# Second attention of a fused convolution-attention kernel: its accumulators move to other PSUM banks, its first blocks run earlier, and two transposed rows are split earlier

## What is computed

```python
def _L1_attn_ref(x):                       # x: tokens after layer norm, (16, 1024, 256)
    xn = x / (jnp.linalg.norm(x, axis=-1, keepdims=True) + EPS)
    scores = jnp.einsum('bid,bjd->bij', xn, xn)
    scores = scores * scores
    weights = jax.nn.softmax(scores, axis=-1)
    context = jnp.einsum('bij,bjd->bid', weights, x)
    return context

x = _L0_conv_ref(x, ...)                   # group norm, q/k/v, softmax attention, projection, residual
t = _to_tokens(x)
t = t + _L1_attn_ref(_ln_t(t))             # the second attention
t = t + _L1_ffn_ref(_ln_t(t), L1_ffn_weight, L1_ffn_bias)
x = _from_tokens(t, x)
```

## Time and profile before

| | |
|---|---|
| median of three runs | 1754.06 us |
| the profiled execution: time, span of its trace | 1754.25 us, 1752.5 us |
| PE busy | 1678.9 us (96%) |
| DVE, ACT, POOL busy | 1359.3, 995.6, 778.3 us |
| mean granted TensorE clock | 0.997 of full speed |
| DMA | 228.40 MB, mean 130 GB/s |

### The profile page before, as it was taken

How to read it: one execution, slowest core, us unless ns; L and a number is a source line. 1 busy time by engine, 2 the same in 40 slices (tenths; PEclk the granted TensorE clock), 3 DMA queues, 4 the chain that set the end, 5 groups by cost and what they waited for, 6 DMA issues and landing times.

```text
span 1752.5 us, 33771 instructions
## 1 busy us (share of the span) xinstructions
PE 1678.9 (96%) x11234; PEld 1527.6 (87%) x11234; DVE 1359.3 (78%) x2597; ACT 995.6 (57%) x1556; POOL 778.3 (44%) x1206
## 2 busy tenths in 40 slices
PE   7999999999999999999999999999999999999996
PEld 6888889888888988889888998888988888898886
DVE  7768777787777877778787777877778777887775
ACT  3565646556465565745647466574655646456572
POOL 1362535526254372634626345253542725337161
PEclk9999999999999999999999999999999999999998
DMA  4634525355252643526344263452535525353342
GB/s 130 168 109 137 154 88 167 103 158 161 82 157 88 191 132 105 150 82 197 112 130 137 92 180 108 144 152 87 162 101 167 156 84 151 99 182 107 109 131 62
DMA packets 197150, 228.40 MB, mean 130 GB/s; under 512 B 27776, under 2 KB 170496, under 8 KB 197120
## 3 DMA queue, kind: packets, MB, share of 16 engines
q1 hardware_dynamic: 197120, 228.01, 43.8%
HBM read 123.08 MB, written 104.86 MB: 130 GB/s over the span
## 4 chain that ended last, share of the span: by engine, by line
issue 27%; POOL 25%; PE 19%; DVE 9%; ACT 8%; DMA 7%; SPq 2%; POOLq 1%; DVEq 0%; ACTq 0%
PE wide L456 10%; POOL e_back L1432 4%; POOL ln_r L1393 4%; POOL prob L1427 3%; DMA e_scratch<-x_norm 3%; DMA e_back<-e_scratch 3%; PE turn L662 3%; POOL val L1419 3%; PE narrow L456 2%; ACT expo L808 2%; POOL xn_lo L1383 2%; PE turn L653 2%; SPq L386 2%; DVE x_norm L1097 2%; DVE prob L1102 1%
## 5 line engine op out<-in xcount | busy, mean ns | idle before, releaser
L456 PE MATMUL wide<-xn_hi,prob 128*128 128x512 f32 x1024 | 305.2, 399 | 3.0 <-DVE prob L1080 3.0
L456 PEld LDWEIGHTS wide<-xn_hi,prob 128*128 128x128 f32 x1024 | 185.2, 188 | 44.7 <-DVE prob L1080 6.3
L815 ACT ACTIVATE prob<-e_back 128x1024 fp32r<-128x1024 f32 x112 | 118.3, 1057 | 144.3 <-DMA e_back<-e_scratch 144.3
L1443 POOL TENSOR_TENSOR carrier_p<-ones 128x1 f32<-128x1 f32 x60 | 11.7, 195 | 417.2 <-DVE y_sb L1185 414.7
L808 ACT ACTIVATE expo<-wide,neg_max 128x1024 f32<-128x1024 f32 x128 | 142.5, 1113 | 73.6 <-DVE neg_max L1090 73.3
L1097 DVE STREAM_TRANSPOSE x_norm<-expo 128x1024 f32<-128x1024 f32 x112 | 139.2, 1243 | 41.7 <-ACT expo L808 41.3
L619 PE MATMUL narrow<-val,prob 128*128 128x258 f32 x512 | 146.7, 287 | 25.9 <-DVE prob L1160 25.9
L1102 DVE TENSOR_TENSOR prob<-e_back,prob 128x1024 fp32r<-128x1024 f32 x112 | 136.1, 1215 | 36.9 <-ACT prob L815 36.9
L1090 DVE TENSOR_REDUCE neg_max<-wide 128x1 f32<-128x1024 f32 x128 | 155.3, 1213 | 11.9 <-PE wide L456 10.0
L1427 POOL TENSOR_TENSOR prob<-expo,prob 128x128 fp32r<-128x128 f32 (+6 forms) x112 | 146.7, 1321 | 39.5 <-DVE prob L1137 39.5
L456 PE MATMUL wide<-xn_lo,prob 128*128 128x512 f32 x512 | 160.7, 394 | 0.0
(11 more groups left out here) (178 smaller groups left out, 5450.9 us busy)
## 6 DMA issues: line engine op xcount, KB each, us to landing
e_scratch<-x_norm SPq DMA_DIRECT2D x112, 512.0 KB, 3.0
e_back<-e_scratch SPq DMA_DIRECT2D x448, 128.0 KB, 3.2
x_raw<-in_x SPq DMA_DIRECT2D x32, 512.0 KB, 3.9
e_back<-in_x SPq DMA_DIRECT2D x64, 256.0 KB, 5.0
out<-y_sb SPq DMA_DIRECT2D x64, 256.0 KB, 3.0
e_scratch<-x_norm SPq DMA_DIRECT2D x32, 448.0 KB, 2.6
x_tok<-e_scratch SPq DMA_DIRECT2D x128, 112.0 KB, 2.6
e_scratch<-x_norm SPq DMA_DIRECT2D x16, 384.0 KB, 2.9
```

Source lines behind the costliest of these rows:

```text
L456: mm = pe.matmul(o, lhsT, r, start=first and i == 0, stop=last and i == len(parts) - 1)
```

## The change

The four accumulators `out2` were the two narrow banks and half of each wide tensor. Now they are the first narrow bank, the two banks of `turn`, and the second narrow bank. The products therefore need no longer wait for the squares that read `wide`, and the next image's queries wait for the squares and not for the residuals.

Three of the pair's 16 blocks ((n, j) = (0, 0), (0, 1) and (1, 1), nine matmuls) run in `front`, between the score pieces 3 and 4. The rest of the pair runs j = 2 to 7, with block (1, 0), the one that reads transposed row 1, just ahead of j = 6.

On ACT, `exp2` is cut into `square2` and `exp2`; the transposed tokens of group 2 (`cosT_hi`) go between the square and the exponential of piece 2, and `e2T_hi` of rows 1 and 2 goes ahead of pieces 7 and 8. On DVE, `e2T_lo` of rows 1 and 2 goes ahead of the splits of row 7. The last image's tail uses other banks for its first half. POOL's and SP's queues keep their order.

```diff
-        out2 = [narrow[0], narrow[1], wide[0][:, 0:BANK], wide[1][:, 0:BANK]]
+        out2 = [narrow[0], turn[:, 0:BANK], turn[:, BANK:N], narrow[1]]
...
-        LAST = dict(ln2T=[turn, wide[1]], y=[y_wide, [narrow[0][:, :], narrow[1][:, :]]], tT=[turn, wide[1]])
+        LAST = dict(ln2T=[wide[1], turn], y=[y_wide, [narrow[0][:, :], narrow[1][:, :]]], tT=[wide[1], turn])
...
-            def product2_pair(b):
-                order = [1, 2, 3, 4, 5, 0, 6, 7]
-                pe.wait_ge(t1_made, NT * b + NT)
-                pe.wait_ge(cosT_made, N1 * b + N1)
+            def products2_begin(b):
+
+                pe.wait_ge(t1_made, NT * b + 6)
+                pe.wait_ge(val_made, N1 * b + 1)
+                pe.wait_ge(p_made, (NT - 1) * b + 2)
+                product2_block(b, 0, 0, 0, 7)
+                product2_block(b, 0, 1, 0, 7)
+                product2_block(b, 1, 1, 1, 7)
+
+            def products2_end(b):
+
                 pe.wait_ge(val_made, N1 * b + N1)
-                for j in order:
-                    if 0 < j < NT - 1:
+                for j in range(2, NT):
+                    if j == NT - 2:
+                        product2_block(b, 1, 0, 1, 7)
+                    if j < NT - 1:
                         pe.wait_ge(p_made, (NT - 1) * b + j + 1)
-                    elif j == NT - 1:
+                    else:
                         pe.wait_ge(p_last_made, 2 * b + 1)
                     for n in (0, 1):
-                        mm = product2_parts(b, n, j, order)
-                        if j == order[-1]:
-                            mm.then_inc(pv2_up, 1)
+                        product2_block(b, n, j, n, 7)
 
             def product2(b, n):
                 if n >= 4:
                     pe.wait_ge(t2_made, NT * b + n - 3)
-                else:
-                    pe.wait_ge(sq2_made, NP * b + NP)
+                elif n == 3:
+                    pe.wait_ge(cosT_made, N1 * b + N1)
...
                 if f is not None:
-                    pe.wait_ge(t2_made, NT * f + NT - 1)
+                    pe.wait_ge(sq2_made, NP * f + NP)
                 queries(b, 0)
-                if f is not None:
-                    pe.wait_ge(t2_made, NT * f + NT)
-                else:
+                if f is None:
                     pe.wait_ge(prep_dve, 8)
                 queries(b, 1)
                 if f is None:
                     pe.wait_ge(prep_dve, 12)
+                else:
+                    pe.wait_ge(t2_made, NT * f + NT)
...
                 scores2(b, 3)
+                products2_begin(b)
                 scores2(b, 4)
...
+                square2(b, 2)
+                cosT_hi(b, 2)
                 exp2(b, 2)
-                cosT_hi(b, 2)
...
+                square2(b, 6)
                 exp2(b, 6)
-                exp2(b, 7)
-                exp2(b, 8)
                 e2T_hi(b, 1)
                 e2T_hi(b, 2)
+                square2(b, 7)
+                exp2(b, 7)
+                square2(b, 8)
+                exp2(b, 8)
...
                 e2_turn(b, 6)
+                e2T_lo(b, 1)
+                e2T_lo(b, 2)
                 e2_hi(b, 7)
                 e2_last_lo(b, 7)
                 e2_hi(b, 8)
                 e2_turn(b, 7)
-                e2T_lo(b, 1)
-                e2T_lo(b, 2)
                 e2_last_lo(b, 8)
```

More of the change, by code:

```diff
@@ L610, in scores2, with product2_block @@
                 three(parts, [wide[J % 2][:, o + s.start:o + s.stop] for s in cuts]).then_inc(s2_up, 1)
-            def product2_parts(b, n, j, order):
+            def product2_block(b, n, j, first, last):
                 if j < n:
@@ L618, in product2_parts @@
                 o = out2[n % 4]
-                pe.matmul(o[:, 0:w], hi, val[:, j, 0:w], start=j == order[0], stop=False)
+                pe.matmul(o[:, 0:w], hi, val[:, j, 0:w], start=j == first, stop=False)
                 pe.matmul(o[:, 0:C], hi, val[:, j, w:w + C], start=False, stop=False, skip_group_check=True)
-                return pe.matmul(o[:, 0:w], lo, val[:, j, 0:w], start=False, stop=j == order[-1])
-            def product2_pair(b):
-                order = [1, 2, 3, 4, 5, 0, 6, 7]
-                pe.wait_ge(t1_made, NT * b + NT)
-                pe.wait_ge(cosT_made, N1 * b + N1)
+                mm = pe.matmul(o[:, 0:w], lo, val[:, j, 0:w], start=False, stop=j == last)
+                if j == last:
+                    mm.then_inc(pv2_up, 1)
+            def products2_begin(b):
[6 more added lines that the diff above has]
+            def products2_end(b):
                 pe.wait_ge(val_made, N1 * b + N1)
-                for j in order:
-                    if 0 < j < NT - 1:
+                for j in range(2, NT):
+                    if j == NT - 2:
+                        product2_block(b, 1, 0, 1, 7)
+                    if j < NT - 1:
                         pe.wait_ge(p_made, (NT - 1) * b + j + 1)
-                    elif j == NT - 1:
+                    else:
                         pe.wait_ge(p_last_made, 2 * b + 1)
                     for n in (0, 1):
-                        mm = product2_parts(b, n, j, order)
-                        if j == order[-1]:
-                            mm.then_inc(pv2_up, 1)
+                        product2_block(b, n, j, n, 7)
             def product2(b, n):
@@ L645, in product2 @@
                 for j in range(NT):
-                    mm = product2_parts(b, n, j, range(NT))
-                mm.then_inc(pv2_up, 1)
+                    product2_block(b, n, j, 0, 7)
             def turn_ln2(f, hf, places=PLACES):
@@ L746, in back @@
             def back(b):
-                product2_pair(b)
+                products2_end(b)
                 for n in range(2, NT):
@@ L763, in _ @@
             f = B - 1
-            product2_pair(f)
+            products2_end(f)
             for n in range(2, NT - 2):
                 product2(f, n)
+            pe.wait_ge(sq2_made, NP * f + NP)
             turn_ln2(f, 0, LAST)
@@ L857, in cosT_hi, with square2 @@
                                ACT.Copy).then_inc(cosT_hi_made, 1)
-            def exp2(b, u):
+            def square2(b, u):
                 J, c0, c1 = PARTS[u]
@@ L871, in exp2 @@
                 act.activation(e, wide[J % 2][:, offset(J) + c0:offset(J) + c1], ACT.Square).then_inc(sq2_made, 1)
+            def exp2(b, u):
+                J, c0, c1 = PARTS[u]
                 act.wait_ge(sq2_made, NP * b + u + 1)
+                e = expo[:, J % DEEP, c0:c1]
                 act.activation(e, e, ACT.Exp).then_inc(e2_made, 1)
@@ L930, in front @@
                 e1T_hi(b, 6)
+                square2(b, 0)
                 exp2(b, 0)
+                square2(b, 1)
                 exp2(b, 1)
@@ L939, in front @@
                 unit_rows(b, 2)
+                square2(b, 2)
+                cosT_hi(b, 2)
                 exp2(b, 2)
-                cosT_hi(b, 2)
                 layer_norm1(b, 3)
+                square2(b, 3)
                 exp2(b, 3)
                 unit_rows(b, 3)
+                square2(b, 4)
                 exp2(b, 4)
@@ L947, in front @@
                 value_rows(b, 3)
+                square2(b, 5)
                 exp2(b, 5)
+                square2(b, 6)
                 exp2(b, 6)
-                exp2(b, 7)
-                exp2(b, 8)
                 e2T_hi(b, 1)
                 e2T_hi(b, 2)
+                square2(b, 7)
+                exp2(b, 7)
+                square2(b, 8)
+                exp2(b, 8)
             def back(b, more):
```

## The result

The changed kernel takes 1737.55 us (median of four runs, 1736.33 to 1739.35) against 1754.94 us of the kernel before in the same comparison: a ratio of 0.9904, 95% interval 0.9887 to 0.9922. It is faster by 17 us, about half of the 34 us that were forecast, and outside the range of 1709 to 1732.

The account below looks back on a forecast made before the run. PE's order bounds the kernel (busy 1678.9 of 1752.5 us). Terms of -1.08, +0.16 and -1.22 give -2.14 us per image, -34.2 over 16 images, from 1754.25 to 1720.0 us; range 1709 to 1732.

Parts of the forecast that it names:

- the three waits: PE's waits before product blocks (25.9 us), turns of the unit tokens (10.2) and a score piece (6.9), all touched.
- Part 1: Between score pieces 3 and 4: a 1.26 us hole swallows nine matmuls, -1.08 us per image.
- The +0.16 at piece 6: PE's score piece 6 starts 0.16 us later per image through later ACT and DVE work, bounds 0 and 0.24.
- Part 2: At block (1, 0): earlier splits of rows 1 and 2 leave 0.63 us in place of 1.85, -1.22 per image.
- B: At block (1, 0): DVE's pair of e2T_lo isn't held, no wait, 2.77 us per image, 1710 us; 15%.
- Part 3: Accumulators and tail: dropped waits on squares and residuals, and the tail's new banks, are worth nothing.
- rival E: Product matmuls writing the turn banks cost over 22 ns more each, so slower; 1766 us at 30 ns; 4%.
- The sum: Whole kernel: -1.08 + 0.16 - 1.22 = -2.14 us per image, -34.2 us over 16 images, 1720.0 us.
- the check of row 4: At tile 3: rows 3 and 4 end near 963.1, ahead of need at 964.0; row 4 is at risk.
- C: At tile 3: norm_lo beats row 4 after 0.3 us of drift, PE stands 1.9 us, 1749 to 1751; 10%.
- The prediction's last sentence: It is wrong if POOL's and DVE's instructions meet in another order than in the image studied; no size given.

Follow-up runs that it names:

- experiment 4: The changed kernel with the splits of transposed rows 1 and 2 back at their old places: 1766.38 us, ratio 1.0076.
- experiment 2: The changed kernel with DVE's cast of row 5 made to wait for POOL's value group 3: 1724.18 us, ratio 0.9832.
- experiment 5: The kernel before with only the accumulators' banks, the waits that go with them and the last image's tail changed: 1754.36 us, ratio 1.0001.
- experiment 1: The changed kernel with POOL's first norm_lo of the next image made to wait until rows 3 and 4 are split: 1717.02 us, ratio 0.979.
- Experiments 3: The kernel before with only rows 1 and 2 split ahead of row 7 on ACT and DVE: 1723.05 us, ratio 0.9824.
- experiment 12: The kernel of experiment 1 with ACT's exponential of piece 2 again ahead of the copy of group 2's tokens: 1716.79 us, ratio 0.9777.
- experiment 11: The kernel of experiment 4 with block (1, 0) one place later, ahead of j = 7: 1748.68 us, ratio 0.9958.

## Why the prediction was wrong

**Bound and waits.** Right: PE's order bounds the kernel, and the three waits were the places.

**Part 1, nine matmuls in the hole.** Right in the changed trace: they begin at 935.33, 0.23 behind piece 3, without a wait, piece 4 doesn't wait for `cosT_lo`, and the turn begins 0.3 us behind piece 4's pace, where it was 0.57. The +0.16 at piece 6 is there too: from piece 3's last matmul to the pair it is 11.43 us now and 11.26 before, with the nine inside (11.41 and 11.17 on average over the images, the upper bound of 0.24). What the part is worth depends on the other: alone it gains nothing (experiment 4); beside it, and with `norm_lo` waiting, 1723.05 becomes 1717.02, 0.4 us per image where I had 0.9.

**Part 2, rows 1 and 2.** Right that they are held until POOL ends: 1.53 us for the 128-wide instruction, 249 ns before, and the hold was the better of the two bounds, so B is out. The Trainium skill's rule ("SBUF — State Buffer", "SBUF: two separate sides") agrees with these rows. The size was off: the wait at block (1, 0) and the restart cost 0.30 us in the changed kernel (4.98 us for the pair less 39 x 0.12) and not 0.63, because POOL's row 6 ended 0.3 us earlier, counted from the pair, than I had it: the flip again. In experiment 2, without the flip, the wait alone is 0.57 and with the restart 0.82 (5.50 less 4.68), so 0.63 was 0.2 us per image too little.

**Part 3.** Right: banks and waits are worth nothing (experiment 5), and rival E is out.

**The sum.** -2.14 us per image, against -2.45 at tile 2 in the changed trace. Without the loss behind it (experiment 1) the kernel gained 36.0 us where 34.2 were forecast. That these agree is partly luck: experiment 1 keeps the flip's shorter wait at block (1, 0), which the forecast didn't have. With the order that the forecast assumed (experiment 2) the gain is 28.9 us.

**The step that failed.** It is the sentence "The same 0.24 runs through DVE's and POOL's splits down to POOL's low part of row 6", together with the check of row 4 that took `norm_lo` at 962.75, where it stood. The shift did not run through both engines. POOL's value group 3 moved by 0.23 us, as forecast, but DVE's cast of row 5 by 0.02: it waits for row 5's scores, which stand behind the turn that Part 1 itself had left at its old time. A common shift would have kept the order. POOL had begun value group 3 just 0.04 us ahead of the cast; moved alone, it came second. Row 5 came 1.15 us sooner and `norm_lo` 0.97, row 4 only 0.22, so C's condition, "0.3 us of drift", was met by 0.75 us. I had given C 10%. The prediction's last sentence, that it is wrong if POOL's and DVE's instructions meet in another order, names what happened; its sum has no term for it. Experiments 1 and 2 show both links, from the cast to `norm_lo` and from `norm_lo` to tile 3, each by one added wait. Experiments 3, 4, 5 and 12 tie the flip to the nine matmuls. Without them the cast is held in every image (1578 ns on average with early rows 1 and 2 alone, 1586 with the new banks alone). With them it comes first, whether rows 1 and 2 are late (experiment 4, all images) or the exponential is back in its place (experiment 12, 723 ns, all images but one). That the unequal shift carries it is read from the traces. C's price was 1.9 us per image and measured 1.48, in 14 images: in the last there is no `norm_lo`, and in one other it came late.

Why that other image escaped can be read from the DMA issues of its rows 3 and 4 (the image that escaped, then the one behind it; the last number is the time from issue to landing):

```profile
e_scratch<-x_norm SPq DMA_DIRECT2D x1, 448.0 KB, 4.0
```

```profile
e_scratch<-x_norm SPq DMA_DIRECT2D x1, 448.0 KB, 2.5
```

The write took 1.6 us longer; the fetch, ACT's `norm_hi` and `norm_lo` waited for it in turn, and `norm_lo` came 0.7 us later than in its neighbours, behind row 4. In experiment 4 one image has such a write too (4.6 us), and its row 4 isn't held either. What stays open is why these writes were slow.

## What to carry to other kernels

Where two engines hold each other out, the trace gives an order of arrival with a margin, not a duration to add to. List the pairs whose margin is smaller than the shift that a change makes (here 0.04 us and 0.24 us), and ask of each of the two instructions what it waits for: the order flips when one moves and the other doesn't. Follow both orders, and fix the one you want with a semaphore: a wait put on the engine that had time to spare cost nothing and gave about 19 us. And test the parts of a change alone: one part gave 30 us, and the whole 17.

## What the runs showed of the hardware

A short stop of PE can cost its clock as well. Behind PE's stop of 1.6 us in the kernel before, the ten us that follow are at 1.00 in all 16 images; behind 1.8 us (experiment 11) the mean fell to 0.83 in 4 of 16, behind 2.5 us (experiment 4) in 9 of 16, and each time cost 1.5 us. That the stop brings the fall about is argued from these counts; within one kernel the longer stops aren't the ones with a fall. The cast with one SBUF input is held as the subtraction with two is: 1580 ns on average for row 5 before, 648 after. And POOL is held in turn: value group 3 took 1.53 us behind DVE's cast, 1.20 when it was first.
